# A macaron layer on one core: the first route and the statistics interleaved on VectorE, picks on unscaled logits

## What is computed

```python
x = x + 0.5 * ffn(layernorm(x), router_w, w1, w2)
x = x + attention(layernorm(x), Qw, Kw, Vw)          # causal softmax attention, scores / sqrt(128)
x = x + 0.5 * ffn(layernorm(x), router_w, w1, w2)

def ffn(xf, router_w, w1, w2):                        # 2048 tokens, 8 experts, H = 512
    probs = softmax(xf @ router_w.T)
    topv, topi = top_k(probs, 2)                      # two experts for each token
    topv = topv / (topv.sum(-1) + 1e-9)
    # each token: sum over its two experts of topv * (gelu(xf @ w1[e]) @ w2[e])
```

## Time and profile before

| | |
|---|---|
| median of 3 runs | 309.88 us (307.61 to 309.95) |
| profiled execution | 309.4 us, of which the span of its instructions is 307.4 us |
| busy: PE, DVE, ACT, POOL | 237.9 (77%), 143.2 (47%), 134.6 (44%), 159.8 us (52%) |
| mean granted clock of TensorE | 0.918 of full speed |

### The profile page before, as it was taken

How to read it: one execution, slowest core, us unless ns; L and a number is a source line. 1 busy time by engine, 2 the same in 40 slices (tenths; PEclk the granted TensorE clock), 3 DMA queues, 4 the chain that set the end, 5 groups by cost and what they waited for, 6 DMA issues and landing times.

```text
span 307.4 us, 5717 instructions
## 1 busy us (share of the span) xinstructions
PE 237.9 (77%) x1866; PEld 220.6 (72%) x1866; DVE 143.2 (47%) x561; ACT 134.6 (44%) x258; POOL 159.8 (52%) x192
## 2 busy tenths in 40 slices
PE   5731998999999994996587907899994999999700
PEld 4630888899999992666264706899993999999600
DVE  5898843522111676589846654343110011343305
ACT  3144465465555411662123515456652466664200
POOL 5807406777706754770616760106777765555740
PEclk9999999999999998999577985989999899999965
DMA  7981113325584351220001113121115324322125
GB/s 211 348 218 42 37 60 93 101 70 171 141 154 149 118 132 44 51 54 9 0 0 37 53 52 98 46 64 37 52 59 151 94 77 134 116 73 63 51 69 170
DMA packets 30491, 28.42 MB, mean 92 GB/s; under 512 B 3496, under 2 KB 25008, under 8 KB 30464
## 3 DMA queue, kind: packets, MB, share of 16 engines
q1 hardware_dynamic: 24640, 17.75, 19.3%
q0 software_dynamic: 4768, 9.79, 12.5%
q10 hardware_dynamic: 1056, 0.53, 0.6%
HBM read 15.23 MB, written 12.82 MB: 91 GB/s over the span
## 4 chain that ended last, share of the span: by engine, by line
PE 56%; DVE 18%; POOL 9%; issue 8%; DMA 7%; ACT 1%; POOLq 0%; DVEq 0%; SPq 0%; ACTq 0%
PE bank L1234 22%; PE bank L1220 22%; POOL slots_in L496 7%; DVE xs L1002 3%; PE bank L1208 3%; PE bank L1274 2%; PE bank L1170 2%; PE bank L1277 2%; DVE stats L702 1%; DMA xn_rows<-xn_numbered 1%; DMA xb_first<-xn_rows,row_in 1%; DMA y_rows<-final_rows 1%; DMA xs<-in_L_attn_x 1%; DVE xT_pack L954 1%; PE bank L1153 1%
## 5 line engine op out<-in xcount | busy, mean ns | idle before, releaser
L1220 PE MATMUL bank<-xT_pack,w_block 128*128 128x128 f32 x680 | 95.7, 288 | 3.6 <-DVE xT_pack L954 3.6
L1234 PE MATMUL bank<-w_sb,act 128*128 x680 | 91.1, 281 | 1.5 <-issue 1.4
L1220 PEld LDWEIGHTS bank<-xT_pack,w_block 128*128 128x128 f32 x680 | 88.0, 203 | 4.9 <-DVE xT_pack L954 4.9
L1234 PEld LDWEIGHTS bank<-w_sb,act 128*128 128x128 f32 x680 | 84.1, 196 | 2.3 <-issue 2.3
L580 ACT ACTIVATE act<-bank 128x512 f32<-128x512 f32 x85 | 50.8, 598 | 73.0 <-PE bank L1220 72.9
L574 ACT COPY w_block<-w_sb 128x512 f32 x85 | 51.7, 613 | 16.0 <-issue 9.8
L485 POOL DMA_INDIRECT xb_first<-xn_rows,row_in x39 | 37.2, 953 | 32.1 <-DMA xn_rows<-xn_numbered 12.3
L507 POOL DMA_INDIRECT y_rows<-slots_out,slot_of x32 | 30.2, 943 | 23.3 <-DMA slots_out<-yb_pack 14.1
L496 POOL DMA_INDIRECT slots_in<-xn_numbered,slot_of x32 | 30.8, 961 | 17.4 <-issue 8.8
L954 DVE COPY xT_pack<-bank 128x512 f32<-128x512 f32 (+3 forms) x28 | 15.7, 561 | 50.8 <-PE bank L1208 45.4
L520 POOL DMA_INDIRECT final_rows<-xb_first,row_of x23 | 22.0, 959 | 32.1 <-DVE xb_first L974 26.3
(11 more groups left out here) (165 smaller groups left out, 256.9 us busy)
## 6 DMA issues: line engine op xcount, KB each, us to landing
w_sb<-in_L_ffn_w SPq DMA_DIRECT2D x8, 512.0 KB, 7.8
xb_pack<-slots_in SPq DMA_DIRECT2D x10, 258.0 KB, 2.9
slots_in<-numbered SPq DMA_DIRECT2D x6, 387.0 KB
y_rows<-final_rows SPq DMA_DIRECT2D x8, 256.0 KB, 3.9
slots_out<-yb_pack SPq DMA_DIRECT2D x5, 256.0 KB, 3.5
xs<-in_L_attn_x SPq DMA_DIRECT2D x4, 256.0 KB, 4.0
out<-xs SPq DMA_DIRECT2D x8, 128.0 KB, 1.8
slots_in<-numbered SPq DMA_DIRECT2D x2, 322.5 KB
```

Of the source, the lines that this page charges most:

```text
L1220: mm = nc.tensor.matmul(h_of(c)[:, q * P:(q + 1) * P], w1_block[c % WIDE_BUFS][:, q * P:(q + 1) * P], xT_pack[n % 2][:, j * P:(j + 1) * P] ...
L1234: mm = nc.tensor.matmul(y_ps[n % 2][:, j * D:(j + 1) * D], act[c % WIDE_BUFS][:, q * P:(q + 1) * P], w2_sb[:, bass.ds(at + q * D, D)], sta ...
```

## The change

It has six parts.

- **DVE's opening.** `then` becomes `following`, which issues an operation, hands control back, and waits for it only when it is resumed. The first route and a chain of norm work (rest of the first half's `rstd`, `scale_shifted(0)`, statistics and `rstd` of the second half, `offset_mean`) are then stepped in turns by `zip_longest`; six steps of the chain come ahead. Everywhere else the generators run through as before.
- **Unscaled picks.** `pick` works on the raw logits; the product with `rstd` is left to `scale_shifted`, which multiplies `shifted` behind the picks and only then raises `shifted_ready`. The last route, whose logits need no scale, loses its copy. `slots_of_picks` does both picks in one wide operation each.
- **Second half's rows.** ACT makes all eight tiles ahead of its first weight copy. The copy of `numbered`, which stood there in one piece, is done in four parts beside blocks 8 to 11.
- **Packs.** The sure packs are 1, 1, 2, 2, 3 blocks instead of 1, 2, 3, 3. The row numbers of the second half come one s later.
- **Results of the first half.** `FIRST_COMBINES` and `FIRST_NORMS` change.
- **`place_first`, `place_second`, `route_first`** swap some independent operations.

The core of the diff:

```diff
-SHARED_PACKS = [1, 2, 3, 3] + [1, 2, 3, 4, 4] + [4, 4, 4, 2, 2]
+SHARED_PACKS = [1, 1, 2, 2, 3] + [1, 2, 3, 4, 4] + [4, 4, 4, 2, 2]
...
-        FIRST_ROWS_BESIDE = 6
-        SECOND_ROWS_BESIDE = 2, 3, 4, 5
-        FIRST_FILL = 6
+        FIRST_ROWS_BESIDE = 7
+        NUMBERED_BESIDE = 10, 11, 12, 13
+        NORM_OPS_AHEAD = 6
+        FIRST_FILL = 7
         TURN_W_BESIDE, QK_W_BESIDE = 19, 21
-        FIRST_PIECES = (0, 0, 3, 3, 4, 5, 7, 7, 12, 13, 14, 15)
-        FIRST_COMBINES = (33, 36, 39)
-        FIRST_NORMS = (37, 38, 39, 40)
+        FIRST_PIECES = (0, 3, 4, 6, 7, 8, 8, 12, 13, 14, 15)
+        FIRST_COMBINES = (32, 34, 37)
+        FIRST_NORMS = (35, 36, 38, 39)
...
+            exp_logits(0)
+            sc.wait_ge(logits_ready, 2)
+            nc.scalar.copy(raw_logit[:], early_logit_ps).then_inc(raw_copied, 1)
             sc.wait_ge(xn_ready, GT)
             sc.dma_start(xn_rows[0:GT * P, :].rearrange("(p t) d -> p t d", p=P), xn[0][:]).then_inc(xn_stored[0], 16)
-            exp_logits(0)
+            second_row_tiles()
             sc.wait_ge(w1_in, 16 * E // 2)
...
+            def following(ins):
+
+                ins.then_inc(dve_step, 1)
+                steps[0] += 1
+                own = steps[0]
+                yield
+                dve.wait_ge(dve_step, own)
...
+                yield from following(v.tensor_reduce(top[:], logit, AX, ALU.max))
+                below = v.tensor_tensor(shifted[g][:], logit, per_tile(top[:]), ALU.subtract)
                 if NORM_OF_ROUTE[r] in UNSCALED:
-                    then(v.tensor_tensor(logit[:], raw, per_tile(rstd[:, g * GT:(g + 1) * GT]), ALU.mult))
+                    yield from following(below)
                 else:
-                    then(v.tensor_copy(logit[:], raw))
-                then(v.tensor_reduce(top[:], logit[:], AX, ALU.max))
-                v.tensor_tensor(shifted[g][:], logit[:], per_tile(top[:]), ALU.subtract).then_inc(shifted_ready, 1)
+                    below.then_inc(shifted_ready, 1)
...
+            def scale_shifted(r):
+
+                g = r % GROUPS
+                v.tensor_tensor(shifted[g][:], shifted[g][:], per_tile(rstd[:, g * GT:(g + 1) * GT]),
+                                ALU.mult).then_inc(shifted_ready, 1)
+                yield True
...
-                for k, chosen in enumerate((pick1, pick2[g])):
-                    then(v.tensor_tensor(work[:], slot[:], chosen[:], ALU.mult))
-                    then(v.tensor_reduce(slot_f[:, k, :], work[:], AX, ALU.add))
+                every_slot = slot[:].rearrange("p t e -> p (t e)").unsqueeze(1).to_broadcast([P, TOP, GT * E])
+                yield from following(v.tensor_tensor(slot_of_pick[:], every_slot, picks[g][:], ALU.mult))
+                yield from following(v.tensor_reduce(slot_f[:], slot_of_pick[:].rearrange("p k (t e) -> p (k t) e", e=E),
+                                                     AX, ALU.add))
...
                 yield from pick(r)
+                if NORM_OF_ROUTE[r] in UNSCALED:
+                    yield from scale_shifted(r)
...
-            rest(rstd_of(0, GT))
-            first_stats(1, range(2))
...
+            norms = chain(rstd_of(0, GT), scale_shifted(0), first_stats(1), rstd_of(GT, GT), scaled_means())
+            for _ in range(NORM_OPS_AHEAD):
+                next(norms)
+            for _ in zip_longest(route_first(), norms):
+                pass
```

More of the change, by code:

```diff
@@ L13 @@
 from contextlib import ExitStack
-from itertools import chain
+from itertools import chain, zip_longest
 import concourse.bass as bass
@@ L129, in macaron @@
         key, logit2, work = sb("key", [P, GT, E]), sb("logit2", [P, GT, E]), sb("work", [P, GT, E])
-        pick1, pick2 = sb("pick1", [P, GT, E]), [sb(f"pick2{g}", [P, GT, E]) for g in range(GROUPS)]
+        slot_of_pick = sb("slot_of_pick", [P, TOP, GT * E])
+        picks = [sb(f"picks{g}", [P, TOP, GT * E]) for g in range(GROUPS)]
         picked16 = sb("picked16", [P, GT, E], BF16)
@@ L811, in place_first @@
[L811 to L815 removed]
+                yield from following(v.tensor_tensor(first_block[:], last, n_full[:], ALU.subtract))
@@ L840, in place_second @@
-                yield
+                yield from following(v.tensor_tensor(n_rest[:], count_ps, spare[:], ALU.add))
+                v.tensor_tensor(beyond[:], ranks, over_tiles(room[:]), ALU.is_ge)
+                yield from following(v.tensor_tensor(over[:], n_rest[:].unsqueeze(2).to_broadcast([P, E, GT]),
+                                                     block_end[:], ALU.is_gt))
+                v.tensor_tensor(slot[:], ranks, over_tiles(shared_base[:]), ALU.add)
+                yield from following(v.tensor_reduce(more[:], over[:], AX, ALU.add))
@@ L1053, in attend, with first_stats @@
                     finish(*units[u])
-            def first_stats(g, tiles):
-                for t in tiles:
+            def first_stats(g):
+                for t in range(GT):
                     if t % HALF == 0:
@@ L1109, in _ @@
             for _ in range(3):
-                next(pieces)
+                next_part(pieces)
             copy_values(1)
```

259 lines of the change are left out of this document (127 added, 132 removed).

## The result

The changed kernel takes 314.4 us, median of 4 runs (313.23 to 314.65); the kernel before, beside it, 309.91 (307.61 to 310.57). The ratio is 1.017, interval 1.0136 to 1.0204: slower by 4 to 6 us. The forecast was 314.3. The profiled executions are 309.4 (span 307.4) before and 313.23 (span 311.2) after, so the trace of after is that of the shortest of its runs, and it explains 3.8 of the 4.5.

The account below looks back on a forecast made before the run. PE held 56% of the chain that ended last, with waits at four touched places; −3.5 + 4.4 + 1.7 + 2.3 = +4.9 on 309.4 gave 314.3, range 309.0 to 316.0 (forecast's own 312.6 to 316.0).

Parts of the forecast that it names:

- Opening, −2.8 at the first product: DVE's opening: second picks 3.7 earlier, ACT takes part back, first expert product at 28.0 instead of 30.83.
- The walk: DVE's new opening order added up operation by operation, 0.26 per chain link and 0.14 to 0.18 per slipped-in instruction.
- Later gathers, −3.5: POOL's gathers for blocks 9 on wait for `row_in`, starting at 43.5 instead of 47.07; bounds 2.9 and 5.3.
- FIRST_COMBINES, +4.4 and +1.7: Block 35: combines ahead of the token copy start it 4.4 later; the idle lowers PE's clock, costing 1.7 more.
- the quick-gathers rival: At block 35 the eighth gather lands in 2.5 and the clock stays up: 2.4 + 0, total 310.6; chance 0.20.
- Route 2, +2.7 and −0.4: Route 2: exponential waits for the late product, +2.7; wide slot operations save 0.4; POOL's scatter moves by +2.3.
- At nothing: Numbered copies and smaller packs, hidden by waits for gathers, counted as no cost; route 3's lost copy at most −0.3.
- Nothing overlaps on DVE: Rival: each DVE operation takes its whole length; second picks at 33.5, first product at 34.3, total 320.3; chance 0.05.
- Both new waits covered: Rival: POOL's result gathers move ahead, leaving only the opening and slot gains, total 305.5; chance 0.10.
- clock rises early: Rival: PE's clock rises soon after the first products, later gathers start at 41.8, 5.3 earlier, total 312.5; chance 0.13.

Follow-up runs that it names:

- b2: The changed kernel with the statistics in sequence instead of interleaved with the first route; 314.14 us, ratio 1.0186 to the kernel before.
- c3: The changed kernel with the second half's rows made beside the first gelus again; 310.67 us, ratio 1.0041 to the kernel before.
- a4: The kernel before with only the first phase's combines and norms moved to their new places; 314.72 us, ratio 1.018 to the kernel before.
- a1: The changed kernel with the first phase's combines and norms back at their old places; 308.33 us, ratio 0.9981 to the kernel before.
- b3: The changed kernel with the fill transfers moved behind the stores of packs 11 to 14; 308.52 us, ratio 1.0014 to the kernel before.
- b1: The changed kernel with 14 instead of 6 statistics steps ahead of the first route; 311.69 us, ratio 1.0092 to the kernel before.
- a3: The changed kernel with ACT's route 2 exponential behind the copies of nT and the projection; 309.8 us, ratio 1.0004 to the kernel before.

## Why the prediction was right, point by point

- *Opening, −2.8 at the first product:* −2.43. The mechanism held: the statistics ride in the first route, and the gain comes behind it. The walk ran ahead of the trace, though. `row_in` came 1.0 later than walked (23.47 for 22.5) and the second `picked` 1.2 later (27.61 for 26.4). A slipped-in operation cost 0.07, not 0.14 to 0.18; `row_in` still came late, so the walk counted too few of them: b2 has `row_in` at 20.97 with none riding along, and 22.5 leaves room for only some 11 of the 37 at 0.14. The first product was to come from ACT at 28.0; it follows PE's ranks instead. On ACT two errors cancelled, the offset's start 0.9 later than walked and the reload of up to 0.97 not there ahead of the weight copy, but this no longer set the time. So the 28.0 was close in part by luck.
- *Later gathers, −3.5:* −2.72, a little below the lower bound of 2.9. The release by `row_in` was right. What it was put down to was wrong: c3 shows that the gathers wait for the same release with the rows made beside the gelus, and that the rows' early store delays the first gathers' landing by 1.1 to 1.6 and the later gathers' start by 1.5. I had counted when this store ends, and not what lands beside it. I had also called the slow first products a matter of the clock; the profile's granted clock is 1.00 in those windows, before as after, while a product of after takes 1.8 to 2.05, so what makes them slow isn't shown.
- *FIRST_COMBINES, +4.4 and +1.7:* +3.54 and +1.64. The place, the order of the waits and the clock behind it were as forecast; a4 makes the loss alone and a1 takes it away. The mis-sized term is the landing of the eighth gather: 3.42 and not 4.5. That it hangs on the fills is shown by b3 (2.73), as the quick-gathers rival needed; with the idle at 2.12 the clock kept.
- *Route 2, +2.7 and −0.4:* the exponential moved by 2.73 against the route's first operation (that moved by 3.07, from 150.65 to 153.72, the exponential by 5.80), the ranks' way to the scatter shortened by 0.38 (4.00 to 3.62). Two things were not in the sum, and both are the clock: the transposes and the projection behind the phase took 0.98 longer (5.74 to 6.72), at 0.50 until 128 rather than 124 in a stretch that starts 2.1 later, and the projection behind route 2 ran 0.86 shorter (6.55 to 5.69). Window of before behind the phase, columns as above:
```profile
124.00:126.00 2.00, 2.00 (x16) 1.70 (x16) 0.49 (x1) 1.43 (x2) 1.44 (x2) 0.97 0.21 51
```
Windows of after:
```profile
122.00:124.00 2.00, 1.49 (x5) 1.24 (x6) 0.94 (x4) 0.37 (x1) 1.39 (x3) 0.50 0.18 47
124.00:126.00 2.00, 2.00 (x4) 0.70 (x3) 0.00 (x0) 0.81 (x2) 1.70 (x2) 0.50 0.27 66
126.00:128.00 2.00, 2.00 (x8) 1.48 (x7) 0.00 (x0) 0.94 (x2) 1.39 (x3) 0.50 0.12 33
```
That route 2 came out at +2.5 is partly the luck of this one execution: in a1, b1, b2 and b3, with the same order, it takes only 0.9 to 1.5 more than before (43.21 to 43.88 against 42.35).
- *At nothing:* the second phase is 0.77 shorter, 0.34 of it by the four-block token copy at 201.52 (34.20 behind the scatter instead of 34.54); 0.25 of this is the lost copy of route 3, for which I had allowed 0.3. The rest stays open.
- *Nothing overlaps on DVE* fell plainly: the second picks came at 27.61, not at 33.5. The price of a slipped-in operation was 0.07, where most of these operations last 0.15 to 0.28. The page "VectorE: DVE Perf Modes" of the Trainium skill says in the section "The DRAIN you can't avoid" itself that a next operation that isn't held starts earlier, and sends the reader to "Two Vector instructions with no wait between them"; the trace agrees with that, and the sentence on the pipe that empties is not to be taken alone.
- *Both new waits covered*, *clock rises early*: neither happened.

So the total, 314.3 for 314.4, is better than its terms. The sum was made on the profiled execution, and that moved by 3.8, to 313.23, not by 4.9: the early gain was 0.8 smaller and the stall 0.9 smaller, which cancel, but the small terms that I had not counted come to about −1.0. The median of after lies 1.2 above its profiled execution, and that brings it to the forecast. The places and the order of the waits were foreseen; the last microsecond is luck.

## What to carry to other kernels

Before moving a wait earlier in an engine's program, look at what stands behind it: here one pair of combines, put ahead of a copy that TensorE needed, cost more than all the gains of the change. An instruction whose result is needed much later (the exponential) doesn't belong ahead of copies that another engine waits for. And a bulk transfer that nothing waits for still has a price when it runs beside others that something waits for: 2.28 against 3.60 for a store, 2.4 to 3.2 against 3.5 to 4.7 for a gather.

## What the runs showed of the hardware

- The loss of clock behind nearly the same idle of PE (the difference in "35 on") differs from kernel to kernel: 1.64 behind 3.89 (after), 2.7 behind 4.18 (a4), 2.9 behind 3.60 (b1), 1.65 behind 2.42 (a3), but nothing behind 3.19 (c3) or 2.12 (b3). The length of the idle alone doesn't settle it, and these are single executions; what does is open.
- A small VectorE operation put between two that depend on each other costs 0.07 (b2: 2.50 for 37) to 0.08 (b1: 0.57 for seven).
- PE's own sequence of blocks is slowed beside the fills (8.32 against 7.58 for a pack of four), although no product waits for these transfers. In the changed kernel one such pause, of 0.48 before a second product at 82.13, has no releaser in the trace, in a stretch with a DMA share of 1.07; what is short there isn't shown.
